# Edge products of a graph layer split over two row halves of TensorE, with two double-bank slots of sums and 264 picks

## The reference

```python
features = H[id_Xe[0]]                                  # x[src], 200000 x 64
M_in = jnp.concatenate([features, Xe], axis=1)
Y = jax.nn.relu(M_in @ M_W.T + M_b)                     # message of each edge
Z = jax.ops.segment_sum(Y, id_Xe[1], num_segments=H.shape[0])
U_in = jnp.concatenate([H, Z], axis=1)
H_next = jax.nn.relu(U_in @ U_W.T + U_b)
...
x = _layernorm(x + H_next)
```

## Time and profile before

| what | value |
|---|---|
| median of 3 runs | 1653.75 us |
| profiled execution, its own time | 1653.16 us |
| its span, first to last instruction | 1651.4 us |
| PE busy | 1602.5 us (97%) |
| DVE busy | 1337.4 us (81%) |
| POOL busy | 1231.4 us (75%) |
| ACT busy | 338.0 us (20%) |
| mean granted TensorE clock | 0.991 |

### The profile page before, as it was taken

How to read it: one execution, slowest core, us unless ns; L and a number is a source line. 1 busy time by engine, 2 the same in 40 slices (tenths; PEclk the granted TensorE clock), 3 DMA queues, 4 the chain that set the end, 5 groups by cost and what they waited for, 6 DMA issues and landing times.

```text
span 1651.4 us, 50341 instructions
## 1 busy us (share of the span) xinstructions
PE 1602.5 (97%) x18218; PEld 1542.1 (93%) x18218; DVE 1337.4 (81%) x1376; ACT 338.0 (20%) x665; POOL 1231.4 (75%) x1312
## 2 busy tenths in 40 slices
PE   5899999999999999999999999999999999999995
PEld 5899999999999999999999999999999999999992
DVE  5788888788787888888888888878788888888863
ACT  4431111112111211211111111112111121111113
POOL 6777777777777777777777777777777777777773
PEclk9999999999999999999999999999999999999997
DMA  8333332323232333333333233333333333333322
GB/s 175 72 72 73 70 78 66 76 66 77 64 79 66 76 73 71 71 71 73 72 70 78 65 76 71 72 68 73 75 69 72 72 70 72 73 72 71 73 48 44
DMA packets 175754, 120.72 MB, mean 73 GB/s; under 512 B 105013, under 2 KB 153882, under 8 KB 175504
## 3 DMA queue, kind: packets, MB, share of 16 engines
q0 software_dynamic: 41216, 42.27, 14.1%
q1 hardware_dynamic: 105810, 56.86, 13.2%
q10 hardware_dynamic: 28478, 18.34, 4.7%
HBM read 114.14 MB, written 3.20 MB: 71 GB/s over the span
## 4 chain that ended last, share of the span: by engine, by line
POOL 69%; issue 23%; PE 5%; DVE 1%; ACT 1%; ACTq 0%; DMA 0%; POOLq 0%; DVEq 0%
POOL gathered L398 69%; PE p_pick L949 2%; PE p_messages L1000 1%; PE p_messages L956 1%; PE p_messages L932 0%; DVE XZ L698 0%; POOL Y L428 0%; PE p_edges_T L914 0%; PE p_edges_T L882 0%; PE p_messages L871 0%; PE p_messages L937 0%; PE p_pick L846 0%; DVE most L646 0%; ACT block_start L494 0%; DVE least L645 0%
## 5 line engine op out<-in xcount | busy, mean ns | idle before, releaser
L398 POOL DMA_INDIRECT gathered<-Y_rows,src_all x1245 | 1175.2, 944 | 379.6 <-issue 379.3
L949 PE MATMUL p_pick<-Y_parts,onehot_src 128*128 128x192 bf16 x12495 | 1061.9, 246 | 6.8 <-DVE onehot_src L755 5.8
L949 PEld LDWEIGHTS p_pick<-Y_parts,onehot_src 128*128 128x128 bf16 x12495 | 1035.7, 98 | 11.5 <-issue 8.2
L755 DVE TENSOR_TENSOR onehot_src<-p_dve,block_start 128x6272 bf16<-128x6272 int16 x255 | 867.0, 3421 | 6.5
L520 ACT COPY edges_T<-p_edges_T 128x512 f32<-128x512 f32 x196 | 114.6, 585 | 973.8 <-PE p_edges_T L914 969.0
L956 PE MATMUL p_messages<-onehot,messages 128*64 128x72 f32 x3126 | 239.4, 230 | 7.7 <-ACT messages L540 7.7
L956 PEld LDWEIGHTS p_messages<-onehot,messages 128*64 128x64 f32 x3126 | 210.2, 138 | 31.7 <-ACT messages L540 8.5
L932 PE MATMUL p_messages<-w_edges,edges_T 128*128 128x128 f32 x1564 | 213.3, 279 | 3.9 <-ACT edges_T L520 3.9
L739 DVE TENSOR_TENSOR p_messages<-p_messages,gathered 128x512 f32<-128x512 f32 x191 | 133.3, 698 | 93.0 <-DMA gathered<-Y_rows,src_all 73.7
L932 PEld LDWEIGHTS p_messages<-w_edges,edges_T 128*128 128x128 f32 x1564 | 190.9, 192 | 5.3 <-ACT edges_T L520 3.4
L540 ACT ACTIVATE messages<-p_messages 128x512 f32<-128x512 f32 x196 | 117.0, 597 | 299.7 <-DVE p_messages L739 296.5
(11 more groups left out here) (98 smaller groups left out, 179.5 us busy)
## 6 DMA issues: line engine op xcount, KB each, us to landing
row_tile<-Y_rows SPq DMA_DIRECT2D x2560, 0.2 KB
edges<-in_edge_attr_dram SPq DMA_DIRECT2D x190, 192.0 KB
gathered<-Y_rows,src_all POOLq DMA_INDIRECT x1245
edges<-in_edge_attr_dram SPq DMA_DIRECT2D x191, 64.0 KB
src_spread<-in_src_dram ACTq DMA_DIRECT2D x65, 128.0 KB
src_spread<-in_src_dram ACTq DMA_DIRECT2D x125, 64.0 KB
Y_rows<-Y SPq DMA_DIRECT2D x6, 256.0 KB
out_dram<-Y SPq DMA_DIRECT2D x6, 256.0 KB
```

Source lines behind the costliest of these rows:

```text
L398: nc.gpsimd.indirect_dma_start(out=gathered[c % G][0:parts, j * D:(j + 1) * D], out_offset=None, in_=table, in_offset=bass.IndirectOffsetO ...
L755: nc.vector.tensor_tensor(onehot_src[k % SLOTS][:, :, :], sources.unsqueeze(1).to_broadcast([P, NW, P]), block_start[:, :, :], ALU.is_equa ...
L949: last = nc.tensor.matmul(p_pick[k % 2][:, 0:3 * D], onehot_src[k % SLOTS][:, b, :], Y_parts[:, b, :], start=(b == 0), stop=(b == NW - 1))
```

## The change

The products of even tiles are made by 64 x 64 parts of `w_edges` in rows 0 to 63 of the array, those of odd tiles in rows 64 to 127, alternately. Each half writes to a bank of its own, so a slot of `p_messages` is two banks and there are two slots in place of three; `p_bc` becomes the second bank of slot 1, which is used outside the chunks only. `add_rows` and `rectify` read and write the two banks as one pattern, by halves. PE waits for `add_window` of chunk c-2 in place of c-3. The chunks that pick two tiles become 74 of 190: 264 picks, and 9 gathers fewer.

```diff
     SLOTS = 3
+    PAIR = 2
...
-        return [TILES - 2, TILES - 1] if c % 3 == 0 or c % 72 == 4 else [TILES - 1]
+        return [TILES - 2, TILES - 1] if c % 9 in (0, 3, 6) or c % 18 == 8 else [TILES - 1]
...
-        p_messages = [pb(f"p_messages{u}") for u in range(SLOTS)]
+        p_messages = [pb(f"p_messages{u}", 2) for u in range(PAIR)]
+        p_halves = [[p_messages[u][:, h * 512:(h + 1) * 512] for h in range(2)] for u in range(PAIR)]
+        p_x_T = p_halves[0] + p_halves[1][0:1]
+        p_bc = p_halves[1][1]
         p_dve = pb("p_dve")
-        p_bc = pb("p_bc")
...
+        def sums_of(c, pairs):
+
+            return p_messages[c % PAIR][:, :].rearrange("p (h n) -> p h n", h=2)[:, :, 0:pairs * D].rearrange(
+                "p h (q d) -> p h q d", d=D)
+
+        def by_halves(rows, pairs):
+
+            return rows[:, 0:pairs * P].rearrange("p (q h d) -> p h q d", h=2, d=D)
...
-                nc.scalar.activation(messages[c % SLOTS][:, 0:pairs * P], p_messages[c % SLOTS][:, 0:pairs * P],
+                nc.scalar.activation(by_halves(messages[c % SLOTS], pairs), sums_of(c, pairs),
...
-                    nc.vector.tensor_tensor(sums, sums, gathered[c % G][:, 0:cols], ALU.add).then_inc(s_rows_added, 1)
+                    nc.vector.tensor_tensor(sums, sums, by_halves(gathered[c % G], pairs), ALU.add
+                                            ).then_inc(s_rows_added, 1)
...
-                if c >= SLOTS:
-
-                    pe.wait_ge(s_chunk_added, c - SLOTS + 1)
+                if c >= PAIR:
+
+                    pe.wait_ge(s_chunk_added, c - PAIR + 1)
                 pe.wait_ge(s_edges_T_copied, c + 1)
-                for q in range(pairs):
-                    last = nc.tensor.matmul(p_messages[u][:, q * P:(q + 1) * P], edges_T[u][:, q * P:(q + 1) * P],
-                                            w_edges[:, :], start=(q == 0), stop=(c >= X and q == pairs - 1))
+
+                def add_products(rows_T, weights, first, final):
+                    for q in range(pairs):
+                        for h0 in range(2):
+                            part = slice(h0 * D, (h0 + 1) * D)
+                            last = nc.tensor.matmul(p_halves[c % PAIR][h0][:, q * D:(q + 1) * D],
+                                                    rows_T[part, q * P:(q + 1) * P], weights[part, part],
+                                                    start=(first and q == 0), stop=(final and q == pairs - 1))
+                    return last
+
+                last = add_products(edges_T[u], w_edges, True, c >= X)
                 if c < X:
                     pe.wait_ge(s_x_rows_T_copied, c + 1)
-                    for q in range(PAIRS):
-                        last = nc.tensor.matmul(p_messages[u][:, q * P:(q + 1) * P], x_rows_T[:, q * P:(q + 1) * P],
-                                                w_gathered[:, :], start=False, stop=(q == PAIRS - 1))
+                    last = add_products(x_rows_T, w_gathered, False, True)
                 last.then_inc(s_summed, 1)
```

More of the change, by code:

```diff
@@ L121, in sb, with pb @@
             return ctx.enter_context(nc.sbuf_tensor(name, shape, dt))
-        def pb(name):
-            return ctx.enter_context(nc.psum_tensor(name, [P, 512], fp32))
+        def pb(name, banks=1):
+            return ctx.enter_context(nc.psum_tensor(name, [P, banks * 512], fp32))
         Y_rows = nc.dram_tensor("Y_rows", [N, D], fp32, kind="Internal").ap()
@@ L211, in gnn_residual_layernorm_kernel @@
         p_x_rows_T = p_pick[1]
-        p_update_T = p_messages
+        p_update_T = p_x_T
         p_update = p_Y
@@ L215, in gnn_residual_layernorm_kernel @@
         p_match = [p_dve[:, P + u * P:P + (u + 1) * P].bitcast(i32) for u in range(2)]
-        p_windows = [p_messages[u][D:P, 0:WIN] for u in range(SLOTS)]
+        p_windows = [p_messages[u][D:P, 0:WIN] for u in range(PAIR)]
         s_ident = sem("s_ident")
@@ L510, in _ @@
                 nc.scalar.copy(x_pairs_T[0:rows, b0 // 2 * W:(b0 // 2 + pairs) * W],
-                               p_messages[g % SLOTS][0:rows, 0:pairs * W]).then_inc(s_x_copied, 1)
+                               p_x_T[g % SLOTS][0:rows, 0:pairs * W]).then_inc(s_x_copied, 1)
                 if g >= 2:
@@ L726, in add_rows @@
                 dve.wait_ge(s_summed, c + 1)
+                pairs = PAIRS if c < NC else TQ
+                sums = sums_of(c, pairs)
                 if c < X:
-                    sums = p_messages[c % SLOTS][:, :].rearrange("p (t d) -> p t d", d=D)
-                    nc.vector.tensor_tensor(sums, sums, m_bias[:, :, :].to_broadcast([P, TILES, D]),
+                    nc.vector.tensor_tensor(sums, sums, m_bias[:, :, :].unsqueeze(1).to_broadcast([P, 2, PAIRS, D]),
                                             ALU.add).then_inc(s_rows_added, 1)
                 else:
-                    cols = (TILES if c < NC else TT) * D
                     dve.wait_ge(s_gathered[c % G], gathered_by(c))
@@ L737, in add_rows @@
                         dve.wait_ge(s_pick_summed, picks_of[c][-1] + 1)
-                    sums = p_messages[c % SLOTS][:, 0:cols]
-                    nc.vector.tensor_tensor(sums, sums, gathered[c % G][:, 0:cols], ALU.add).then_inc(s_rows_added, 1)
+                    nc.vector.tensor_tensor(sums, sums, by_halves(gathered[c % G], pairs), ALU.add
+                                            ).then_inc(s_rows_added, 1)
             def copy_match(c):
@@ L762, in add_window @@
                 columns = XZ[D:P, bass.ds(start, WIN)]
-                nc.vector.tensor_tensor(columns, columns, p_windows[c % SLOTS], ALU.add).then_inc(s_chunk_added, 1)
+                nc.vector.tensor_tensor(columns, columns, p_windows[c % PAIR], ALU.add).then_inc(s_chunk_added, 1)
             def add_all_windows(c):
@@ L769, in add_all_windows @@
                     columns = XZ[D:P, bass.ds(w * WIN, WIN)]
-                    nc.vector.tensor_tensor(columns, columns, p_windows[c % SLOTS],
+                    nc.vector.tensor_tensor(columns, columns, p_windows[c % PAIR],
                                             ALU.add).then_inc(s_window_added, 1)
@@ L870, in transpose_x @@
                     n = min(2, b1 - b)
-                    last = nc.tensor.transpose(p_messages[g % SLOTS][0:n * D, (b - b0) // 2 * W:((b - b0) // 2 + 1) * W],
+                    last = nc.tensor.transpose(p_x_T[g % SLOTS][0:n * D, (b - b0) // 2 * W:((b - b0) // 2 + 1) * W],
                                                xb[:, b:b + n, :].rearrange("p n d -> p (n d)"), ident[:, :])
@@ L955, in sum_window @@
                 for j in range(tiles):
-                    last = nc.tensor.matmul(p_windows[u], messages[u][:, j * D:(j + 1) * D],
+                    last = nc.tensor.matmul(p_windows[c % PAIR], messages[u][:, j * D:(j + 1) * D],
                                             onehot[u][:, j, :], start=(j == 0), stop=(j == tiles - 1))
```

## The result

The changed kernel takes 1700.68 us (median of 4 runs, 1697.71 to 1702.04) against 1653.76 before: slower, ratio 1.0281, 95% interval 1.0263 to 1.0299. The range of the prediction held it; the predicted 1727 us was 26 too high. The profiled execution took 1697.71 us, its span is 1695.9.

A forecast was written before the change was run, and what follows sets the result against it. PE and POOL were taken to bound the kernel together. Picks and end (+22.3 us) plus products (196 x 0.26 = 51.0) gave +73.3 on 1653.16, 1726.5, stated as 1727 us; range 1685 to 1878 us.

The forecast's parts named there:

- The two bounds and the picks: PE and POOL both bound; nine picks cost PE 36.4 us, less 9.6 slack and 4.5 at the end: +22.3 us.
- The load sets the pace: Products on PE: loading 128 stationary columns takes about 0.108 us, however few rows or moving columns.
- the two halves load side by side: Products on PE: loads for lower and upper rows overlap, x between 0.05 and 0.08 us; chance 0.42.
- The entry: From the picks' end to the first 64-row product's end on PE: 0.25 us, against 0.14 before.
- The pace: Time x per 64-row product record on PE: 0.062 us taken, products ending 0.25 + 15x after picks, 0.26 more per chunk.
- the kept bound of 0.054: Lower floor of x, both halves loading wholly side by side: 0.054 us per product record, 1703 us in all.
- One load after another: Rival: the halves' product loads take turns at 0.112 us, nothing overlaps; +220 us, 1874 us; chance 0.34.
- The faster one: Rival: product halves run at their moving columns' pace, 0.057 us a couple; POOL's 11.2 us gained, 1642.6 us; chance 0.21.
- PE's wait for the window add: Rival: with two slots, PE's products wait for DVE's window add; 190 us at 1 us a turn; no chance given.
- The two-bank patterns: DVE's add and ACT's relu over two banks: 0.6 to 1.4 us each, hidden beside the 4.05 us pick, costing nothing.
- The row of 16: Sign: a chunk's 16 product records take 1.2 to 1.35 us; near 2 us means serial loads, under 0.9 faster.
- if they still wait for issue alone, PE isn't the bound: Sign: POOL's gathers should wait 70 us or more for DVE's row adds; waiting only for their own issue refutes PE's bound.

The follow-up runs named there:

- experiment 1: Kernel before with only the new list of picks (264), products over all 128 rows, three slots: 1676.14 us, ratio 1.0130.
- Experiment 4: Kernel before with 264 picks, full chunks' products with 64 moving columns in place of 128, all rows, odd tiles left out of sums: 1666.07 us.
- experiment 6: Kernel before with 264 picks, window sums of even and odd tiles in separate column halves, odd sums left out of XZ: 1644.13 us.
- experiment 5: Changed kernel with the products of the four even tiles first, then the four odd ones: 1797.72 us, ratio 1.0862.
- experiment 7: Kernel before with window sums in two column halves, both added by DVE: 1645.41 us with 264 picks, 1639.88 with 273, 1637.14 with 275 and no neighbouring two-pick turns.

## Why the prediction was right, and where it was off

**The two bounds and the picks: right.** PE had 9.6 us of slack, POOL's gain of 11.2 us was never paid out, and the picks cost 22 us by themselves (+22.3 predicted, 22.0 measured in experiment 1). The +22.3 counts 4.5 us won at the end, and the windows of chunk 194 came 4.4 us sooner after its products.

**The load sets the pace: right.** It rested on one pair of records at 33 us. Experiment 4 shows it from the other side, with the rows kept and the moving columns halved. That the two halves load side by side was a choice among cases, put at 0.42; no row of before could tell it.

**The entry: right.** 0.25 us from the end of the picks to the end of the first product were taken from the earlier trace rows; they are 810.33 + 0.33 - 810.40 = 0.26, against 0.14 before. With 7 x 0.111 behind it this is the whole 1.04, so the 0.12 us by which a turn grew is the entry alone. The load's row shows the place: `[0.16 <-issue]`, PEld idle ahead of the first pair, 192 times and 30.9 us in all.

**The pace: the mis-sized term.** I set x = 0.062 us, "the larger of two floors, since it is the quickest row there is for this couple". That floor doesn't exist: two records of different halves start 7 ns apart, and 0.062 us was the windows' own pace, with 72 moving columns, which experiment 6 keeps for a pair. The measured pace per record is 0.111/2 = 0.056 us. In the terms of the sum, 0.25 + 15x = 1.04, x comes to 0.053, since 16 records make 7 steps between pairs and not 7.5. That is the kept bound of 0.054, with which the working gave 1703 us; 1700.7 was measured. In the turn the products cost 0.118 us more in place of 0.26. The 0.14 us between them, 196 times, are 28 us; the miss is 26.

**The rules.** The Trainium skill, "TensorEngine Tiling (Array Packing)", Key Properties, on tiles that load and multiply in parallel: the trace agrees, two loads in 0.19 us. Its Theoretical Speedup gives up to 2x where a dimension is 64 or less. The rows show none of it for the products (contraction 64), where the load of 128 columns is as long as before, and nearly all of it for the windows of experiment 6 (64 stationary columns), 0.72 us in place of 1.21.

**The rivals.** One load after another (0.34) fell: even in experiment 5 the halves overlap. The faster one (0.21) fell with the result, and experiment 4 shows why: it priced the pair by its moving columns. PE's wait for the window add is 2.5 us. The two-bank patterns cost nothing: DVE's 0.70 us and ACT's 0.60 are unchanged.

**The signs named beforehand.** The row of 16 takes 1.11 us (forecast 1.2 to 1.35), the turn 6.81 (6.95): each off by the same x. POOL waits 32 us for the row adds (70 or more), and x alone doesn't explain that, for it took off 26 us of PE's excess only. The rest went into POOL's lead, which the forecast had left out. Its last gather starts at 1624.46 us, 31.5 us before chunk 194's products, and had started 8.4 us after them, so some 40 us of what PE lost went into that lead. The waits for row adds up to 1000 us:

```profile
POOL gathered L412 <- DVE p_messages L752: 1.2, 4, 0.3
```

The sign "if they still wait for issue alone, PE isn't the bound" was a wrong one for the same reason: in experiment 1 PE is the bound, and POOL waits 3.4 us.

The mean granted clock is 0.991 as before, its upper level through the turns (1.00 from 100 to 1600 us).

## What to carry to other kernels

Before a matmul is split over halves of the array, ask which is longer per record, the load of its stationary columns or its moving columns, and read the load's price from the first two loads of a row. The steady pace can't tell: here both sides stood at 0.111 us. This row split halved the moving columns, since `w_edges` is block-diagonal, and left each half as many loads as before, so there was nothing to gain, and it paid for a change of shape besides (0.12 us a turn). By the same reasoning it would gain where the moving side is the longer; for halves by columns experiment 6 shows that, for halves by rows no run does. Work given to an engine on the strength of an expected gain (here 9 picks) should wait until the turn's length shows the gain.

## What the hardware showed that was not expected

Records of different halves start 7 ns apart, so nothing in PE's issue stood at 0.062 us. With 8 records of one half queued before those of the other, PE started the second half in the middle of the first: matmuls later in the program ran beside earlier ones, and 16 records took 1.60 us, between 1.11 (alternating) and about 2 (in turn, an estimate).

A short wait of PE can cost about twice its length: after waits of 2.00 and 1.92 us (experiment 7) the granted clock sank for a few us, and the picks behind them took 1.6 us longer. Both traces show it in a turn with two picks.

The changed kernel's runs spread over 4.3 us, those of before beside them over 0.2 (2.4 over 13 runs beside the first experiments). The longer the run, the lower its mean granted clock at the two ends: 0.991 at 1697.71 us and 0.989 at 1702.04, and with 255 picks 0.994 at 1661.53 and 0.987 at 1666.96. The turns of the two traces don't differ (6.81 us). The start does: with 255 picks and the split, chunk 4's products started at 64.91 us in place of 61.75, and the granted clock from 56 to 64 us was 0.69 there against 1.00 (busy time by stage, the last numbers of each row: clock, DMA share, GB/s; first the changed kernel, then the one with 255 picks):

```profile
56.00:64.00 8.00, 6.42 (x93) 6.03 (x94) 5.58 (x8) 4.34 (x9) 6.17 (x7) 1.00 0.41 103
```

```profile
56.00:64.00 8.00, 6.21 (x57) 5.75 (x55) 3.80 (x7) 3.25 (x5) 6.17 (x7) 0.69 0.23 54
```

In both, PE ran at the lower level (0.50, 1.2 GHz) from 40 to 48 us. So it did in experiment 5, the third trace with the split, where chunk 4's products start at 67.07 us. In the eight traces without it the clock of that stretch is 0.79 to 0.95, and chunk 4's products start between 60.55 and 61.99 us. So two of the three split traces lose 3 to 6 us at the start as well, beyond anything in the turns. Why the clock comes back sooner in one execution than in another, and whether this accounts for the whole spread, is open.
